# Clears of a spare tile on GpSimd in front of the row scatters and result scatters of a fused attention and expert kernel

## The reference, cut

```python
x = x + tanh(g_xattn[0]) * xattn(ctx_2048, layernorm(x), mask, mask, ...)     # 8 heads of 16
x = x + tanh(g_ffn[0]) * ffn(layernorm(x), ...)

def ffn(x, ...):                      # 2048 tokens, 9 experts, 352 hidden
    scores = sigmoid(x @ gate.T + bias)
    top_scores, selected = top_k(scores, 2)
    top_scores = top_scores / (sum(top_scores) + 1e-20)
    for e in range(9):
        h = silu(x @ w1[e].T) * (x @ w3[e].T)
        out = out + cw[:, e:e+1] * (h @ w2[e].T)
```

## Time and profile before

| | us |
|---|---|
| three timed runs | 217.81, 218.2, 218.67 |
| the profiled execution, span from its first to its last instruction | 234.1 |
| PE busy in the span | 205.4 (88%) |
| DVE busy | 149.6 (64%) |
| ACT busy | 142.7 (61%) |
| POOL busy | 128.8 (55%) |
| POOL in row scatters, 32 | 32.7 |
| POOL in result scatters, 38 | 37.8 |
| POOL in clears of `spare`, 24 | 4.9 |

### The profile page before, as it was taken

The page is one execution under the profiler, slowest core; times in us unless marked ns, Lnnn a source line. Parts: engine busy times, 40 slices in busy tenths (PEclk is TensorE's granted clock), DMA queues, the critical chain, the costliest instruction groups (busy, mean ns, idle before and its releaser), DMA issues.

```text
span 234.1 us, 5788 instructions
## 1 busy us (share of the span) xinstructions
PE 205.4 (88%) x1606; PEld 166.9 (71%) x1606; DVE 149.6 (64%) x523; ACT 142.7 (61%) x399; POOL 128.8 (55%) x230
## 2 busy tenths in 40 slices
PE   8999986999999999898883946299999999999981
PEld 3577653666666676565573945299999999999881
DVE  0469997788898698897865822344443444456774
ACT  2286869988778876786471620266667666666210
POOL 4237745132325876786783578556675756557320
PEclk9999999999999999999998897589999999999998
DMA  5999999999910100011372221121222221261194
GB/s 164 368 377 242 407 381 409 408 370 318 342 55 13 36 23 26 23 36 38 86 214 62 61 76 49 41 53 55 61 69 68 52 65 47 49 218 53 37 348 163
DMA packets 23602, 34.91 MB, mean 149 GB/s; under 512 B 2562, under 2 KB 15879, under 8 KB 23443
## 3 DMA queue, kind: packets, MB, share of 16 engines
q1 hardware_dynamic: 20610, 29.27, 37.9%
q0 software_dynamic: 2240, 4.23, 5.5%
q10 hardware_dynamic: 720, 1.02, 1.5%
HBM read 15.85 MB, written 19.06 MB: 149 GB/s over the span
## 4 chain that ended last, share of the span: by engine, by line
PE 56%; DVE 14%; another core or an unknown queue 7%; ACT 6%; DMA 6%; issue 5%; POOL 4%; SPq 1%; POOLq 0%; DVEq 0%; ACTq 0%
PE pt_ps L1363 10%; PE score_ps L1321 5%; PE pt_ps L1372 4%; PE score_ps L1323 4%; PE score_ps L1322 4%; PE score_ps L1176 4%; DMA kheads<-y_rows 3%; PE pt_ps L1116 3%; PE ps_a L1226 3%; PE pt_ps L1214 3%; PE score_ps L1126 2%; PE ps_b L1283 2%; DVE less L827 2%; ACT probs L401 2%
## 5 line engine op out<-in xcount | busy, mean ns | idle before, releaser
L616 POOL DMA_INDIRECT y_rows<-vals,ids x38 | 37.8, 995 | 17.2 <-ACT vals L473 9.6
L1363 PE MATMUL pt_ps<-w,probsT 128*128 x234 | 34.4, 285 | 14.6 <-ACT probsT L480 6.7
L1363 PEld LDWEIGHTS pt_ps<-w,probsT 128*128 128x128 f32 x234 | 32.1, 198 | 15.9 <-issue 15.8
L593 POOL DMA_INDIRECT x_rows<-stage,slot x32 | 32.7, 1022 | 10.4 <-issue 7.7
L401 ACT ACTIVATE probs<-score_ps,less 128x128 f32<-128x128 f32 x128 | 37.9, 419 | 0.4 <-DVE less L827 0.4
L1043 DVE TENSOR_TENSOR xg_low<-ps_a,xg_high 128x128 fp32r<-128x128 f32 x40 | 11.7, 291 | 37.1 <-issue 23.6
L473 ACT ACTIVATE vals<-pt_ps,xg 128x128 f32<-128x128 f32 x38 | 14.0, 368 | 34.4 <-PE pt_ps L1363 24.7
L1321 PE MATMUL score_ps<-w_high,xg_low 128*128 x80 | 30.3, 379 | 0.0
L1051 DVE TENSOR_TENSOR probs<-probs,score_ps 128x352 f32<-128x352 f32 x40 | 20.8, 521 | 11.2 <-PE score_ps L1323 5.3
L1323 PE MATMUL score_ps<-w_high,xg_high 128*128 x80 | 26.6, 332 | 0.0
L1322 PE MATMUL score_ps<-w_low,xg_high 128*128 x80 | 26.5, 332 | 0.0
(11 more groups left out here) (179 smaller groups left out, 445.6 us busy)
## 6 DMA issues: line engine op xcount, KB each, us to landing
x_rows<-pads SPq DMA_DIRECT2D x1, 9945.0 KB, 37.3
w_low<-in_w13T SPq DMA_DIRECT2D x3, 1056.0 KB, 11.0
xg<-x_rows SPq DMA_DIRECT2D x40, 65.0 KB
ctx_r<-in_ctxT SPq DMA_DIRECT2D x4, 512.0 KB, 7.7
y_rows<-pads SPq DMA_DIRECT2D x1, 2048.0 KB, 16.6
w<-in_w2T SPq DMA_DIRECT2D x1, 1728.0 KB, 11.2
kheads<-y_rows SPq DMA_DIRECT2D x3, 512.0 KB, 5.0
mask_b<-in_mask SPq DMA_DIRECT2D x4, 256.0 KB, 8.0
```

Source lines behind the costliest of these rows:

```text
L593: pool.indirect_dma_start(x_rows[:, :], bass.IndirectOffsetOnAxis(ap=slot[:, par, c, p:p + 1], axis=0), stage[:, par, c, p, :], None, boun ...
L616: pool.indirect_dma_start(y_rows[:, :], bass.IndirectOffsetOnAxis(ap=ids[:, s:s + 1], axis=0), yt[:, s, :], None, bounds_check=last_row, o ...
L1363: last = nc.tensor.matmul(into[:, 0:D], hidT[:, q3, c, :], w2[:, bass.ds(e3, 1), c, :].rearrange("p o d -> p (o d)"), start=(c == 0), stop ...
```

## The change

The spare tile grows from 384 to 768 columns of bf16. `scatter` calls `space(768)` in front of each indirect DMA for the groups 2 and 3: 16 clears of 768 columns. `tile` calls `short_space()` for all 38 result scatters, and no longer for the first 24 only: 14 more clears of 128 columns.

```diff
+SPACE = 6 * D
-        ... spare = ... sb("spare", [P, 3 * D], BF16)
+        ... spare = ... sb("spare", [P, SPACE], BF16)
...
                 for c in copies:
+                    if g >= NG - 2:
+                        space(SPACE)
                     pool.indirect_dma_start(x_rows[:, :], ...)
...
-                if k < 3 * TR:
-                    short_space()
+                short_space()
                 pool.wait_ge(y_done, k + 1)
```

More of the change, by code:

```diff
@@ L95, in build @@
         share = sb("share", [P, P], BF16)
-        minus_half, minus_one, spare = sb("minus_half", [P, UN]), sb("minus_one", [P, UN]), sb("spare", [P, 3 * D], BF16)
+        minus_half, minus_one, spare = sb("minus_half", [P, UN]), sb("minus_one", [P, UN]), sb("spare", [P, SPACE], BF16)
         xs = sb("xs", [P, NB, D])
```

## The result

The changed kernel takes 227.38 us (median of 4 runs, 226.47 to 228.33) against 218.0 for the kernel before in the same comparison: 1.0415 times as long, 95% interval 1.0365 to 1.0465, some 9.4 us. The prediction said 225.8.

The account below looks back on a forecast made before the run. Without the profile's waits PE's tiles set the pace, POOL close behind; 16 wide clears make POOL last. Moving tile 37's scatter costs 7.0 to 8.3 us, 7.6 taken on 218.2: 225.8 us, range 215.5 to 231.5.

Parts of the forecast that it names:

- The waits: Five unexplained chain pieces between 121 and 150 us, 16.45 us, taken to belong to the profiled execution, not the timed runs.
- The price of a clear: On POOL, 768 columns take 0.74 us; row scatters come every 1.95 instead of 1.28 us, 0.67 more for each of 16.
- Delays DVE and PE by a good microsecond, which tile 8's wait swallows: In group 2, the last block's variance comes behind two clears; the delay disappears in tile 8's wait.
- Tile 8's wait: Tile 8 waits for group 2's last scatter, moved from 123.67 to 129.0, and can start at 133.5.
- PE loses 3.2 us there: At tile 16, behind group 3's last scatter: start at 152.4 instead of 149.2, without the waits.
- POOL becomes the last by 4.5 us: At the end, POOL's scatter of tile 37 starts at 208.6, PE's result is there at 204.1.
- I book no gain: 14 new short clears, 0.21 us each, counted within the 1.65 of result scatters; no gain booked as POOL no longer waits.
- The sum: Loss on tile 37's scatter: 7.0 us, or 8.3 if POOL set it before; 7.6 taken, giving 225.8 us.
- The end hangs on that scatter: At tile 37's result scatter: once it has landed, 16.0 us follow until the last instruction.
- Waits in the timed runs: Rival: timed runs hold the waits and the clears end them; 208.8 us, or 217.0 with half of them; chance 0.20.
- A cheap clear: Rival: the clear costs 0.21 us or is hidden, POOL's chain grows by 1.4 us; 217.1 to 219.3 us, chance 0.08.
- PE held up by tighter trains: Rival: 36 result scatters every 1.65 us bring waits that hold PE; 232, up to 238 us, chance 0.10.

Follow-up runs that it names:

- the two profiles with the low clock: Kernel before with short clears for all 38 result scatters and no wide ones, 218.33 us; kernel before without any clear, 218.38 us.
- without their hold: Kernel with wide clears in group 2 alone, three of DVE's instructions rewritten with a second input from SBUF: 222.55 us, 1.0186.
- one run: Changed kernel with wide clears in front of group 3's row scatters only: 223.23 us, 1.0249.

## Why the prediction was right, and where its terms were off

**The waits.** Right: a second profile of the same code has none, and spans 216.0. What decided was the arithmetic of span against median. It compared unlike things, though: span and time differ by 1.8 us in every timed run, so that 217.65 stood against a span of 216.4 and not against 218.2, and the profiled execution was 17.7 us longer than the median, not 15.9. The 1.2 us left over lie in a profile whose clock was 0.82 from 120 to 158 us (1.00 in the second one). The rule on the notification block that the prediction cited from the Trainium skill ("NOTIFIC — the notification-queue block", section 7.1) made the same call; but the second profile holds as many instructions (5788) and no such wait, so how the waits came about stays open.

**The price of a clear.** 0.753 us for 0.74. The cycle was 2.00 for 1.95, since the gap from a clear to its scatter is 0.28, not the 0.17 to 0.26 that I took. Sixteen times 0.05 is 0.8 us, and the places on POOL are off by that: group 3's last scatter 148.67 for 147.9, tile 37's 209.42 for 208.6. Behind the train two smaller misses nearly cancel: 35 turns of 1.64 instead of 1.65 save 0.35 us, and the slow scatters of tiles 33 to 35 cost 0.4 more than the slow copies that I had counted.

**"Delays DVE and PE by a good microsecond, which tile 8's wait swallows".** Too small. PE was 3.4 us late at tile 8 (2.4 to 2.5 against the two profiles with the low clock) and no load was waited for. The variance ended 1.4 us late (118.00 for 116.63), and most of the rest came with three instructions of DVE that stood until a clear ended; without their hold tiles 5 to 7 came 1.2 to 2.0 us earlier. I had priced a clear by what it takes from POOL alone. Tile 8's wait (133.5 forecast) was there underneath: with the hold taken away it showed at 134.15.

**"PE loses 3.2 us there" (tile 16).** Mis-sized. In the undisturbed kernel before, tile 16 starts at 147.59, not at 149.2, for PE gains where my subtraction left gaps; in the changed one at 153.82, not at 152.4, since group 3's last scatter came 0.8 us later and from it to the tile it took 5.15 us instead of 4.49 (6.0 in one run; why is open). PE loses 6.2 us, or 5.2 to 5.4 against the two profiles with the low clock.

**"POOL becomes the last by 4.5 us".** Right in kind: 3.7 us. As PE was later than I thought, less of the loss is POOL's own: by the profiles PE alone brings 5.4 to 6.5 us, and POOL the rest. For the sum this miss did no harm, since POOL's chain ends behind PE's either way.

**"I book no gain", the 14 short clears.** Wrong. I had them within the 1.65, and set against it 1.72 for a scatter without one, so that they cost nothing. My 1.72 came from rows where POOL waits for results; in a backlog it is 1.50. They cost 1.2 us by the medians, and 2.65 us on tile 37's scatter (209.42 for 206.77).

**The sum.** 7.6 us forecast, 9.4 measured. On the scatter of tile 37: 0.8 us from the clear's cycle, and 1.0 because before it starts at 199.98, not at some 201 (the mean of 201.6 and 200.3). PE, not POOL, sets it there: the run without clears shows it. That the scatter's move is the kernel's loss was luck in part. "The end hangs on that scatter" holds in the changed kernel, but in the undisturbed kernel before the end is DVE's; it happens to come 16.0 us behind the scatter's start there, and 16.8 in the changed kernel. (The 16.0 us of the prediction, too, count from the scatter's start, 218.06, not from its landing.)

**The rivals.** Waits in the timed runs: excluded. A cheap clear: holds for 128 columns (1.003), not for 768 (1.0415). PE held up by tighter trains: no unexplained piece in the changed kernel's chain.

## What to carry to other kernels

Hold the span of the profile against the timed runs before reading any wait in it; where they differ by more than the spread, profile once more. Price work on one engine twice: by what it adds to that engine's chain up to the next point where another waits, and by what it keeps from running beside it. And take the pace of a backlog from rows where the engine really has one.

## What was not expected of the hardware

- Three instructions of DVE with a single input from SBUF took 1.07 to 1.24 us instead of 0.16 to 0.34 where a clear came next on POOL, and ended with it; with a second input from SBUF they took 0.15 to 0.25 us. The Trainium skill, "SBUF — State Buffer", section "Who interferes with whom", says that DVE and GpSimd share one pair of ports as an exclusive lock, that `tensor_scalar`, copies and casts can take it, and that an instruction with two SBUF inputs contends only with a GpSimd instruction that reads SBUF. A clear reads nothing, so the forms that stood and those with two inputs agree with it. Not every form that can take the ports stood: casts of one column took 0.15 us within clears of the changed kernel (`ids_in<-xg`, 136.03 us). The page gives the pair to whichever issues first; here DVE's instruction started 0.3 to 0.5 us earlier by the profile and still ended behind the clear, so by these starts, rough as they are on POOL, the trace does not agree.
- PE idle for 1.94 us in one piece came back at a mean clock of 0.72 over the next 6 us. It does not go by the length of that piece alone: 1.36 us of idle ahead of tile 16 in the changed kernel, and 2.24 us there with group 3's clears alone, left the clock at 1.00. At the end, after 5.12 us of waiting, the last eight matmuls of the changed kernel took 2.08 us at a clock of 0.50, where those of the kernel before took 1.16 at 1.00 behind a wait of 1.44.
- A short clear costs 0.14 us in a backlog (1.64 for 1.50), less than its own 0.20.
